# Moving a layer norm's root refinement from VectorE to GpSimd and its scaling to ScalarE, in the first attention of an eight-layer kernel

## The reference, cut to what matters

```python
def _layernorm(x, axis=-1, eps=1e-05):
    m = jnp.mean(x, axis=axis, keepdims=True)
    v = jnp.var(x, axis=axis, keepdims=True)
    return (x - m) / jnp.sqrt(v + eps)

x = x + _L0_attn_a_ref(_layernorm(x, axis=-1), Wq, Wk, Wv, Wo)   # causal attention
x = x + _L0_ffn_ref(_layernorm(x, axis=-1), gate_w, w1, b1, w2, b2, w3, b3, sw1, sw2, sw3)
...
    for e in range(E):                                            # in _L0_ffn_ref
        h = jax.nn.silu(jnp.einsum('tkd,hd->tkh', xs, w1[e]) + b1[e])
        x2 = jnp.einsum('tkh,dh->tkd', h, w2[e]) + b2[e]
        x3 = jnp.einsum('tkd,hd->tkh', xs, w3[e]) + b3[e]
```

## Time and profile before

| | |
|---|---|
| three timed runs | 1176.35, 1181.18, 1181.31 us; median 1181.18 |
| profiled execution | 1176.26 us, of which span 1174.5 us |
| busy in the span | PE 986.9 us (84%), DVE 845.4 (72%), ACT 389.4 (33%), POOL 340.2 (29%) |
| first attention | the first 240 us of the span |
| step 7, step 11, step 15 of its loop | from about 124, 169 and 213 us |

### The profile page before, as it was taken

How to read it: one execution, slowest core, us unless ns; L and a number is a source line. 1 busy time by engine, 2 the same in 40 slices (tenths; PEclk the granted TensorE clock), 3 DMA queues, 4 the chain that set the end, 5 groups by cost and what they waited for, 6 DMA issues and landing times.

```text
span 1174.5 us, 16896 instructions
## 1 busy us (share of the span) xinstructions
PE 986.9 (84%) x6263; PEld 594.0 (51%) x6263; DVE 845.4 (72%) x1985; ACT 389.4 (33%) x638; POOL 340.2 (29%) x346
## 2 busy tenths in 40 slices
PE   8889898679999877779999768999996758987475
PEld 3434444333344656543444336677684545766254
DVE  5588887467766666766776796495675994788895
ACT  2435455423433343323433561122112222321121
POOL 5452232202222433303323501102102333332242
PEclk9899999889999797779999969999999776986796
DMA  5352212020000000000000000000000000000000
GB/s 127 108 171 62 59 46 95 2 94 1 1 1 1 1 1 1 1 1 0 1 1 1 0 1 3 1 1 1 1 1 1 1 1 1 3 1 1 1 10 27
DMA packets 11534, 24.35 MB, mean 21 GB/s; under 512 B 1323, under 2 KB 7635, under 8 KB 11315
## 3 DMA queue, kind: packets, MB, share of 16 engines
q1 hardware_dynamic: 11152, 22.28, 6.5%
q10 hardware_dynamic: 294, 0.91, 0.3%
HBM read 15.68 MB, written 7.34 MB: 20 GB/s over the span
## 4 chain that ended last, share of the span: by engine, by line
PE 58%; DVE 32%; issue 4%; ACT 2%; POOL 2%; DMA 0%; DVEq 0%; ACTq 0%; POOLq 0%
PE ps L908 4%; PE ps L915 4%; PE ps L903 4%; PE ps L328 3%; PE ps L278 2%; DVE a_MN L482 2%; PE ps L2415 2%; PE ps L1951 2%; PE ps L1905 2%; DVE XN L131 2%; PE ps L1948 2%; DVE q_E L1566 2%; PE ps L298 2%; PE ps L1809 2%; PE ps L1237 1%
## 5 line engine op out<-in xcount | busy, mean ns | idle before, releaser
L482 DVE TENSOR_REDUCE a_MN<-ps 128x1 f32<-128x384 f32 (+3 forms) x154 | 93.6, 638 | 26.4 <-PE ps L281 24.9
L1193 POOL TENSOR_TENSOR f_Y<-f_Y,f_TT 128x512 f32<-128x512 f32 x48 | 61.0, 1270 | 138.8 <-DVE f_TT L1062 138.8
L105 POOL TENSOR_TENSOR rs<-t,mhalf 128x4 f32<-128x4 f32 x37 | 37.5, 1014 | 171.7 <-DVE t L94 170.4
L162 DVE TENSOR_TENSOR X<-ps,X 128x512 f32<-128x512 f32 x32 | 22.0, 688 | 90.6 <-PE ps L1961 49.4
L1152 ACT ACTIVATE f_HH<-ps,pack_zero 128x512 f32<-128x512 f32 x64 | 44.0, 688 | 105.4 <-PE ps L903 105.4
L622 ACT ACTIVATE a_PT<-ps 128x1024 f32<-128x1024 f32 x56 | 57.4, 1025 | 59.7 <-PE ps L298 59.5
L908 PE MATMUL ps<-f_XS,pack_zero 128*128 128x512 f32 x128 | 72.6, 650 | 0.0
L1062 DVE SCALAR_TENSOR_TENSOR f_TT<-ps,pack_zero,f_X 128x512 f32<-128x512 f32 x64 | 47.8, 748 | 33.8 <-PE ps L915 33.4
L915 PE MATMUL ps<-f_HH,pack_zero 128*128 128x512 f32 x128 | 66.8, 604 | 4.4 <-DVE f_TT L1062 4.4
L903 PE MATMUL ps<-f_XS,pack_zero 128*128 128x512 f32 x128 | 67.7, 611 | 1.1 <-DVE f_XS L1051 1.1
L2238 PE MATMUL ps<-pack_one,XNT 128*128 128x352 f32 x128 | 49.7, 537 | 22.4 <-DVE q_HH L2287 22.3
(11 more groups left out here) (326 smaller groups left out, 2366.2 us busy)
## 6 DMA issues: line engine op xcount, KB each, us to landing
scratch<-a_parts SPq DMA_DIRECT2D x16, 384.0 KB, 3.3
a_QS<-scratch SPq DMA_DIRECT2D x14, 288.0 KB
a_KS<-scratch SPq DMA_DIRECT2D x42, 96.0 KB
pack_one<-in_one SPq DMA_DIRECT2D x1, 2679.5 KB, 9.4
pack_zero<-in_zero SPq DMA_DIRECT2D x3, 884.5 KB, 4.6
X<-in_x SPq DMA_DIRECT2D x4, 256.0 KB, 10.2
out_x<-X SPq DMA_DIRECT2D x4, 256.0 KB, 2.0
a_QS<-a_MT SPq DMA_DIRECT2D x42, 4.0 KB
```

Source lines behind the costliest of these rows:

```text
L482: dve.tensor_reduce(M.a_MN[:, n % 2, ti, h0:h0 + k], bank(M, M.bank["a_max", n, jj], 128 * (ti + 1) * k).rearrange("p (a c) -> p a c", a=k ...
L1193: pool.tensor_tensor(M.f_Y[:, i, :], M.f_Y[:, i, :], M.f_TT[:, u % 3, :], ALU.add).then_inc(made.sem, made.tick(n, u))
```

## The change

The refinement of the root for batches 0 to 2 moves from DVE to POOL, in a new function `norm_factors` behind the power: four Newton steps, then mean times root and its negation, six instructions, each behind a wait for the one before. The scaling moves from DVE to ACT, as four Identity activations with root and negated product as scale and bias, between exps(n,2) and exps(n,3) of steps 7, 11 and 15. PE's transposes of these batches wait for a new signal `a_normed`, which shares a semaphore with `g_exp`. `expert_bias` moves from the end of step 14 to behind the loop, after normalize(13) and ahead of normalize(14). The fourth batch's norm stays as it was.

```diff
--- before.py
+++ after.py
@@ -19,7 +19,7 @@
 
 SHARED = {"r_proj": "a_proj", "r_scored": "a_scored", "r_valued": "a_valued", "r_u": "a_maxed", "r_read": "a_turned", "r_mean": "a_back",
           "r_ke": "a_parts", "r_pp": "a_reduced", "r_kd": "a_split", "r_qd": "a_mt", "r_ss": "a_on",
-          "r_km": "a_f", "r_v": "a_exped", "r_ot": "a_ol", "r_raw": "a_ot", "f_rowt": "a_rowt", "p_qt": "a_own", "p_ones": "a_mx0"}
+          "r_km": "a_f", "r_v": "a_exped", "r_ot": "a_ol", "r_raw": "a_ot", "f_rowt": "a_rowt", "a_normed": "g_exp", "p_qt": "a_own", "p_ones": "a_mx0"}
 
 
 class Signal:
@@ -103,6 +103,25 @@
     var, root = S["variance"], S["root"]
     pool.wait_ge(var.sem, var.at(n, b))
     pool.tensor_tensor(M.rs[:, 4 * b:4 * b + 4], M.t1[:, 4 * b:4 * b + 4], M.mhalf[:, 0:4], ALU.pow).then_inc(root.sem, root.tick(n, b))
+
+
+def norm_factors(pool, S, M, b):
+
+    root, a, z = S["root"], 4 * b, 4 * b + 4
+    r, t, v, mean = M.rs[:, a:z], M.t2[:, a:z], M.t1[:, a:z], M.mv[:, a:z, 0]
+    pool.wait_ge(root.sem, root.n)
+    pool.tensor_tensor(t, r, r, ALU.mult).then_inc(root.sem, root.tick())
+    pool.wait_ge(root.sem, root.n)
+    pool.tensor_tensor(t, t, v, ALU.mult).then_inc(root.sem, root.tick())
+    pool.wait_ge(root.sem, root.n)
+    pool.tensor_scalar(t, t, -0.5, 1.5, ALU.mult, ALU.add).then_inc(root.sem, root.tick())
+    pool.wait_ge(root.sem, root.n)
+    pool.tensor_tensor(r, r, t, ALU.mult).then_inc(root.sem, root.tick())
+    pool.wait_ge(root.sem, root.n)
+    pool.tensor_tensor(t, mean, r, ALU.mult).then_inc(root.sem, root.tick())
+    pool.wait_ge(root.sem, root.n)
+    pool.tensor_scalar(t, t, -1.0, None, ALU.mult).then_inc(root.sem, root.tick("scale", b))
+    pool.wait_ge(root.sem, root.n)
 
 
 def newton(dve, S, v_, r_, t_):
@@ -447,7 +466,7 @@
             if hh == 2 and g == 2 and b:
                 output(b - 1)
             if hh == 3 and g == 3 and b:
-                turn_tensor(pe, S, M, 1, b - 1, side(M), M.XN, (S["normed"], (1, b - 1)))
+                turn_tensor(pe, S, M, 1, b - 1, side(M), M.XN, (S["a_normed"], (b - 1,)))
     turned(14, 4)
     for si in range(4):
         values(15, si)
@@ -557,18 +576,9 @@
         if n + 1 < 16:
             row_copy(n + 1)
         if more:
-            reduce(n + 2, 5)
-        if left is not None:
-            norm_refine(dve, S, M, 1, left)
-        if more:
-            reduce(n + 2, 6)
-        if left is not None:
-            norm_scale(dve, S, M, 1, left, M.X, M.XN, range(0, 2))
-        if more:
-            reduce(n + 2, 7)
+            for jj in range(5, 8):
+                reduce(n + 2, jj)
         normalize(n - 2)
-        if left is not None:
-            norm_scale(dve, S, M, 1, left, M.X, M.XN, range(2, 4))
         if more:
             reduce(n + 2, 8)
         if g == 2 and b:
@@ -577,8 +587,7 @@
             reduce(n + 2, 9)
             reduce(n + 2, 10)
             maxima_split(n + 2)
-        if n == 14:
-            expert_bias(dve, S, M)
+    expert_bias(dve, S, M)
     normalize(14)
     normalize(15)
     residual(dve, S, M, 0, 3, M.bank["a_out", 3], S["result"])
@@ -644,6 +653,13 @@
             act.wait_ge(S["a_turned"].sem, S["a_turned"].at(n - 2))
         act.wait_ge(S["a_valued"].sem, S["a_valued"].at(n))
         act.activation(M.a_OL[:, n % 2, :], bank(M, 5), ACT.Copy).then_inc(made.sem, made.tick(n))
+
+    def scaled(b):
+
+        made = S["a_normed"]
+        act.wait_ge(S["root"].sem, S["root"].at("scale", b))
+        for t in range(4 * b, 4 * b + 4):
+            act.activation(M.XN[:, t, :], M.X[:, t, :], ACT.Identity, bias=M.t2[:, t:t + 1], scale=M.rs[:, t:t + 1]).then_inc(made.sem, made.tick(b))
 
     def back(b):
         made = S["a_ot"]
@@ -680,6 +696,8 @@
         exps(n, 1)
         tail(n, 0)
         exps(n, 2)
+        if g == 3 and b:
+            scaled(b - 1)
         exps(n, 3)
         tail(n, 1)
         if g == 3 and b:
@@ -736,6 +754,7 @@
         b, g = n // 4, n % 4
         if g == 3 and b:
             norm_root(pool, S, M, 1, b - 1)
+            norm_factors(pool, S, M, b - 1)
         for half in range(2):
             seen(n, half)
     norm_root(pool, S, M, 1, 3)
```

## The result

The changed kernel takes 1167.10 us (median of 7 runs, 1166.26 to 1169.72), the one before 1176.35 us (median of 7 runs, 1172.82 to 1183.69). The medians are 9.25 us apart, a ratio of 0.9921. The ratio of the comparison itself is 0.9904 with a 95% interval of 0.9876 to 0.9931, which is 11.3 us (8.1 to 14.6). In a second comparison on one chip it was 0.9928 (0.9905 to 0.9951), 8.5 us: 1168.46 against 1177.01 us. So the change makes the kernel about 9 us faster, where 7.2 had been summed.

The account below looks back on a forecast made before the run. The prediction took DVE's norm work and the expert bias to lie on PE's chain of waits in the first attention stage. Gains of 2.5 + 3.2 + 1.5 = 7.2 us from 1178.7 gave 1171.5 us, range 1165.5 to 1179.5.

Parts of the forecast that it names:

- Steps 7 and 11: First attention stage, norms of batches 0 and 1: DVE loses refinement and scaling, 2 x 1.25 = 2.5 us gained.
- POOL's steps: Six new 128x4 instructions behind the power: 0.20 us plus 0.08 hop each, 1.7 us in all (1.1 to 6.5).
- The threshold for ACT's wait: In loop steps 7 and 11, ACT begins to wait for POOL from 0.42 us per POOL step.
- The price at which gain turns to loss: In loop steps 7 and 11, the change turns to a loss from about 0.66 us per POOL step.
- rival C: POOL's small steps cost 1.01 us each, delaying ACT's scalings and then the mask: 3.4 to 6.5 us slower; chance 0.06.
- ACT's scalings: Four scalings between exps(n,2) and exps(n,3): 0.46 us each, overlapping, 1.5 us in all (0.8 to 2.4), costed at nothing.
- The end: Loop steps 14 and 15: PE starts turned(14) at 222.05 instead of 225.25, 3.2 us gained (2.3 to 3.9).
- both parts are needed here: End of the stage: the 3.2 us needs norm move and bias move; with the bias left in place, 0.9.
- The clock: Granted-clock fall after step 11 counted as gone, 1.5 us; the second, in 220 to 232, as half kept.
- A: Clock keeps its falls or new ones come: 5.7 us or less gained, 1173.0 up to 1177 us; chance 0.20.
- B: ACT becomes the bound, a scaling costing 0.6 us or more: 4.3 us gained, 1174.4 us; chance 0.12.
- D: Chain turns to another wait, such as POOL's late masks: under 2 us gained, 1177 to 1180 us; chance 0.12.

Follow-up runs that it names:

- 8 steps more: Changed kernel with eight more small GpSimd steps ahead of the one ScalarE waits for, in steps 7, 11, 15: 1172.59 us, ratio 0.9947 to the kernel before.
- 16 steps more: Changed kernel with sixteen more small GpSimd steps ahead of the one ScalarE waits for: 1183.61 us, ratio 1.0045 to the kernel before.
- the change with the copies in the other order: Changed kernel with ScalarE's a_OL copy of group 14 ahead of batch 2's XNT copy: 1167.24 us, ratio 0.9891 to the kernel before.
- the one with the bias alone: Kernel before with only expert_bias moved behind the loop, refinement and scaling staying on VectorE: 1171.78 us, ratio 0.9957.

## Why the prediction was right and wrong

**Steps 7 and 11: right.** 2 x 1.25 us forecast, 1.25 and 1.26 measured at full clock, and the same in all seven profiles with the short wait. The way of reading it, a norm-free step as the measure of what the stretch can become, gave the number, where the 1.88 us of removed DVE work would have been too much.

**POOL's steps: right.** 0.28 us each forecast, 0.28 to 0.29 measured, factors at 129.52 + 1.72 = 131.24 where 1.7 behind the power was forecast. The Trainium skill's rule (GPSIMD Engine Reference, Key points) of a VectorE twice as fast would have made it 0.34 us an instruction, and the trace does not agree for a tile this small: 0.20 us against VectorE's 0.15 to 0.17. The 0.16 us of dispatch that the prediction quotes stands on that page as VectorE's figure and not GpSimd's; no term used it. The threshold for ACT's wait held (8 steps more: 14 x 0.285 = 4.0 us, ACT waits 1.67). The price at which gain turns to loss, 0.66 us per step of six, was a little low: with these 4.0 us the two steps still gain 0.33 and 0.31 us. At 1.05 us per step they lose 2.5 and 2.9 us with the half clock in them, where rival C had 1.7. The wait's path to PE was wrong in rival C: XN's transposes and the XNT copy, not the masks.

**ACT's scalings: a term a little small.** 1.64 us measured, 1.5 forecast. The Trainium skill's formula (ScalarE: Activation LUTs, What ACT_TABLE_LOAD costs) had given 1.64, and the trace agrees with it to the hundredth. It changed nothing in steps 7 and 11.

**The end: the wait right, one claim wrong.** 3.2 us forecast, 3.22 measured from turned(13) to turned(14). That both parts are needed here is half true: the norm's move needs the bias out of the way (0.57 us without it), but the bias does not need the norm's move, it alone gives 3.68. The prediction had not priced it alone.

**The clock: this term failed.** The prediction counted one fall in step 11 as typical and gone (1.5 us), and the fall at the end as half kept. Four profiles of the kernel before show a fall behind step 7 in three and behind step 11 in two, 2.7 us per execution. "Step 7 has the same waits and no fall" was the chance of one profile and no property of the step. No fall follows any of the 14 short waits, so these 2.7 us are spared. But the end gives back 2.1 of them on average: its stretches are only 1.1 us shorter although its wait is 3.2 us shorter, by the fall at the head of step 15 and by more half clock behind turned(14). Net, the profiles show 0.6 us from the clock in this stage, not 1.5.

**The sum and the level: here it failed.** The change moved the median by 9.25 us from 1176.35; I wrote 1171.5 us, which is 4.85 below that. Of the difference 2.35 us are the level: I took the middle between the profiled run (1176.26) and the median of three runs (1181.18), 1178.7, as the time from which to subtract. More runs put the kernel before at 1176.35 and 1177.01. The three runs had two of the slower ones among them. The other 2.05 us are gain that the sum of 7.2 does not have, and they do not come from the falls that it had priced. The sum made against the profiled execution alone, 1169.1, is 2 us from the result. The time was inside the range because that was wide; the size of the change against the true level was not well told.

**Where 9 us come from.** Here the profiles are compared, four of the kernel before and two of the change, whose times differ by 8.7 us on average. From the first residual to the last of the first attention those of before take 113.6, 115.7, 113.3 and 116.5 us (mean 114.8), those of the change 108.6 and 108.4: 6.3 us, which is 5.7 of waits and 0.6 of clock. From there to the last residual of the kernel, where no instruction differs, it is 936.0 against 934.2 on average, 1.8 us; but over all kernels of this study this part scatters from 933.8 (8 steps more) to 939.4 (16 steps more) without order, and the change with the copies in the other order has 937.5. Up to the first residual it is 0.7 us, also in front of anything that the change touches. So 6.3 us are located in the stage, and that the shorter waits spare clock falls is shown in steps 7 and 11. The other 2.5 to 3 us lie outside the stage. Whether the change moves clock falls there, or whether this is scatter, stays open.

**The rivals.** A (falls stay or new ones come, 5.7 us or less) did not come by the timing, but half of its mechanism did: the falls behind steps 7 and 11 went, and one at the head of step 15 came. B (ACT as the bound) holds for the end only, where ACT is the last but still leaves 3.2 us. C needed a step of about 1.05 us and came true when that time was put in. D did not come: every wait that the prediction named fell.

## What to carry to other kernels

Measure what a relieved engine is worth by a neighbouring step of the loop that lacks the extra work, and not by the work removed. Look for the one late call in a queue first: moving the bias behind the loop, out of the way of the next norm, gave 3.7 us of waits with one moved call, more than the whole change has at that place, while moving the norm alone left a new wait of the same kind. And do not read clock falls off one profile: take several, and set the sum against the time of the execution that it was read from. A fall can hide behind a wait, and removing the wait then brings it out, as at the head of step 15.

## What the runs showed of the hardware

Waits of 0.65 and 0.92 us within 2 us, PE busy between them, were followed by a fall to 1.2 GHz in five of ten cases (the kernel before and the one with the bias alone), at 1.5 to 3.1 us each; a wait of 0.49 us in no case of 14; a wait of 2.87 and one of 2.90 us (16 steps more) both times. A 128x4 operation on GpSimd takes 0.20 us, the power of the same size 1.01. In step 15 of the kernel before, VectorE's four 128x4 instructions of the refinement (L110 to L116) took 0.32 to 0.57 us each while GpSimd was masking, and 0.15 to 0.17 in step 7, where it was not. An Identity activation of 128x128 from SBUF with two pointers takes 0.41 us per piece in a row of four, and no table load stands between it and the exponentials: the changed kernel's profile has none from 3.5 to 236.8 us.
